# A graph network's edge stage, worked on 256 edges a step instead of 128

## The reference

```python
h  = relu(layernorm(x))
xn = layernorm(h) * ln_g + ln_b                     # 50000 x 256
q, k, v = xn @ Wq.T + bq, xn @ Wk.T + bk, xn @ Wv.T + bv
dk, dv  = silu(edge_attr @ Wdk.T + bdk), silu(edge_attr @ Wdv.T + bdv)
attn = silu(sum(q[dst] * k[src] * dk, axis=1)) * cosine_cutoff(edge_weight)
agg  = segment_sum(v[src] * dv * attn[:, None], dst)
x1   = x + h + agg @ Wo.T + bo
h1   = relu(layernorm(x1))
# graph convolution over the reversed edges with self-loops and degree norm, then a two-layer head
h7   = segment_sum((h1 @ W)[col] * norm, row) + b
out  = x1 + relu(h7 @ W1 + b1) @ W2 + b2
```

## Time and profile before

| what | value |
|---|---|
| three runs, median (lowest to highest) | 2039.34 us (2038.46 to 2040.52) |
| the profiled execution, own time | 2035.36 us |
| its span, first to last instruction | 2033.7 us |
| preparation, until the edge stage has the degree table | 0 to 118 us |
| edge stage, until its last scatter has landed | 118 to 848 us |
| second stage, until its last scatter | 848 to about 1235 us |
| node stage, overlapping it by a few steps | to 2034 us |
| busy: PE, DVE, ACT, POOL | 82%, 69%, 59%, 68% of the span |

### The profile page before, as it was taken

The page is one execution under the profiler, slowest core; times in us unless marked ns, Lnnn a source line. Parts: engine busy times, 40 slices in busy tenths (PEclk is TensorE's granted clock), DMA queues, the critical chain, the costliest instruction groups (busy, mean ns, idle before and its releaser), DMA issues.

```text
span 2033.7 us, 32020 instructions
## 1 busy us (share of the span) xinstructions
PE 1667.5 (82%) x6331; PEld 1026.7 (50%) x6331; DVE 1406.6 (69%) x5976; ACT 1193.9 (59%) x2320; POOL 1389.7 (68%) x1047
## 2 busy tenths in 40 slices
PE   4939999999999999344444541999999999999999
PEld 2315454445544545233333331676767666666666
DVE  7956666666666666355545547888888888888883
ACT  5925555554555454122222124998898989898884
POOL 2047888888888885488888877666666666666660
PEclk9959999999999999666656655999999999999999
DMA  7996555555555556244445458899999999999991
GB/s 247 418 363 204 142 146 150 140 143 143 154 140 142 145 144 203 47 87 89 89 89 90 87 102 206 234 272 273 263 272 269 269 270 268 272 269 267 266 256 72
DMA packets 170410, 391.76 MB, mean 193 GB/s; under 512 B 38847, under 2 KB 85872, under 8 KB 170368
## 3 DMA queue, kind: packets, MB, share of 16 engines
q1 hardware_dynamic: 105920, 257.96, 37.6%
q0 software_dynamic: 59552, 115.52, 31.0%
q10 hardware_dynamic: 4896, 17.83, 2.2%
HBM read 211.37 MB, written 179.85 MB: 192 GB/s over the span
## 4 chain that ended last, share of the span: by engine, by line
POOL 31%; DMA 22%; PE 18%; issue 16%; DVE 9%; SPq 2%; ACT 1%; POOLq 1%; DVEq 0%; ACTq 0%
POOL sums_dram L480 8%; DMA sums_dram<-ub,sidx 8%; POOL cg L484 7%; DMA out_dram<-cg 6%; POOL kept L567 6%; PE bank L1312 6%; PE bank L1301 6%; POOL b_rs L476 4%; DMA cg<-in_x_dram,ib 4%; PE bank L1169 3%; DVE cg L929 3%; POOL tab_d L484 3%; DMA cg<-sums_dram,ic 3%; POOL rs L476 2%; PE bank L1291 1%
## 5 line engine op out<-in xcount | busy, mean ns | idle before, releaser
L480 POOL DMA_INDIRECT sums_dram<-ub,sidx x196 | 318.9, 1627 | 96.8 <-issue 42.7
L1301 PE MATMUL bank<-kept,w 128*128 128x512 f32 x784 | 354.6, 595 | 0.0
L1312 PE MATMUL bank<-w_sb,kept 128*128 128x256 f32 x1568 | 354.3, 379 | 0.0
L567 POOL TENSOR_TENSOR kept<-kept 128x1024 f32<-128x1024 f32 x98 | 233.4, 2382 | 176.4 <-DVE cg L929 176.4
L1267 PE MATMUL bank<-cg,en 128*128 128x256 f32 x392 | 178.3, 634 | 204.4 <-ACT cg L1074 197.6
L1312 PEld LDWEIGHTS bank<-w_sb,kept 128*128 128x128 f32 x1568 | 297.9, 190 | 81.9 <-issue 46.4
L484 POOL DMA_INDIRECT cg<-in_x_dram,ib x196 | 206.3, 1052 | 78.9 <-issue 58.4
L1267 PEld LDWEIGHTS bank<-cg,en 128*128 128x128 f32 x392 | 120.5, 322 | 262.1 <-issue 236.4
L476 POOL TENSOR_TENSOR b_rs<-b_ve,minus_half 128x8 f32<-128x8 f32 x102 | 209.8, 2057 | 23.7 <-DVE b_ve L946 23.7
L476 POOL TENSOR_TENSOR rs<-ve,minus_half 128x4 f32<-128x4 f32 (+1 forms) x149 | 145.2, 974 | 101.4 <-DVE ve L781 91.6
L1301 PEld LDWEIGHTS bank<-kept,w 128*128 128x128 f32 x784 | 142.2, 191 | 141.9 <-issue 141.8
(11 more groups left out here) (183 smaller groups left out, 3227.7 us busy)
## 6 DMA issues: line engine op xcount, KB each, us to landing
sums_dram<-cg SPq DMA_DIRECT2D x162, 512.0 KB
kept<-in_x_dram SPq DMA_DIRECT2D x97, 512.0 KB, 5.8
kept<-sums_dram POOLq DMA_DIRECT2D x97, 512.0 KB, 9.9
cg<-sums_dram SPq DMA_DIRECT2D x97, 512.0 KB, 8.8
out_dram<-cg SPq DMA_DIRECT2D x97, 512.0 KB, 9.7
sums_dram<-cg ACTq DMA_DIRECT2D x34, 512.0 KB
row_d<-in_dst_dram SPq DMA_DIRECT2D x97, 64.0 KB
...
```

The source lines that it names most:

```text
L480: pool.indirect_dma_start(sums, bass.IndirectOffsetOnAxis(idx, 0), rows, None, bounds_check=last_row, compute_op=ALU.add).then_inc(done, 16)
L567: pool.tensor_tensor(X1[k.slot(8)], X[k.slot(4)], H[k.slot(2)], ALU.add).then_inc(g_xh, 1)
L1301: ins = pe.matmul(bank[:, 2 + m, :], w01[:, c, m * P:(m + 1) * P], hT[k.slot(2)][:, c * GN:(c + 1) * GN], start=(c == 0), stop=(c == KC - 1))
L1312: ins = pe.matmul(to, rT[k.slot(2)][:, c * GN + j * P:c * GN + (j + 1) * P], w2_sb[:, c, :], start=False, stop=(c == KC - 1), skip_group_c ...
```

## The change

The edge stage goes over 49 pairs (EP) of chunks instead of 98 chunks, in 49 + 7 steps instead of 98 + 11.

- POOL's program is written straight out for all 56 steps, with constant wait values. A step gathers four times 128 rows (the destination rows straight into `kept`, where they stay), raises one tile of six variances a partition to the power -0.5 (pair p-2), gathers two table entries (p-1) and issues two scatters (p-7) back to back, after both scatters of the pair before have landed. The index tile `ib` and the copies to it are gone.
- The first normalization is no longer scaled: ACT rectifies x minus its mean, the second layer norm takes that up through its variance, and x + h is formed by one instruction from the rectified rows, their scale and the rows in `kept`. So a pair has one power, after both statistics, instead of two.
- EQ of the second chunk is 256 wide: sums of the first chunk's edges take in the second chunk's messages too, and "first edge" is tested over the pair. Spare rows are two sets of 128.
- The biases sit in row 0 of the q, k, v weights: feature 0 of every normalized row is set to 1 and the row of feature 0 is subtracted from the weights of all features (a layer norm's features sum to zero). The short bias products go. The weights are changed once, in DVE's step 2.
- The edge attributes come turned from the host's array, 64 partitions of 256 edges; the turn on PE and the copy on DVE go. SP loads attributes and destination numbers once a pair, and fills `sums1` twice a pair.
- The copy of the sums out of PSUM moves from DVE to ACT, one for the pair (512 wide), and so does the copy to UB. The product with the table is formed once, behind the stage.
- ACT issues its fills eight a step instead of four. Temporary tiles of the preparation lie at the end of the room of `kept` instead of at its start.

The diff, cut to the loops (the indentation is cut too):

```diff
 assert ROWS - N >= P
-MESSAGE_STEPS = 11
...
-FILLS_STEP = 4
+FILLS_STEP = 8
...
-at0 = taken[0]
+at0 = EC * D - taken[0] - words if taken is early else taken[0]
...
-X2 = [CG[1][:, i, :].rearrange("p (a d) -> p a d", a=2) for i in range(4)]
-H2 = [CG[2][:, i, :].rearrange("p (a d) -> p a d", a=2) for i in range(4)]
+XS = [CG[1][:, i // 2, i % 2 * D:(i % 2 + 1) * D] for i in range(4)]
+G2 = [CG[2][:, i, :].rearrange("p (a d) -> p a d", a=2) for i in range(4)]
...
+    q = k.slot(2)
+    if k.within(EP):
+        wide = E - (EP - 1) * 2 * P if k.reg is None and k.off == EP - 1 else 2 * P
+        if k.past(2):
+            pass_on(sp, (m_D, k.value(-1, 2)))
+        sp.dma_start(aT[q][0:R, 0:wide], edge_attr[:, bass.ds(k.value(0, 2 * P), wide)]
+                     ).then_inc(m_attr[q], 16)
+        if k.past(2):
+            pass_on(sp, (m_eq, k.value(-1)))
+        sp.dma_start(row_d[q][:, 0:wide],
+                     dst[bass.ds(k.value(0, 2 * P), wide)].rearrange("(a e) -> a e", a=1)
+                     .broadcast_to([P, wide])).then_inc(m_row[q], 16)
...
+        for i in range(2):
+            sp.dma_start(sums1[bass.ds(k.value(0, 2 * GN) + i * GN, GN), :]
+                         .rearrange("(p j) d -> p (j d)", j=G), rows_0).then_inc(s_fill1, 16)
...
+def gather_x(p):
+    if p >= 2:
+        pool.wait_ge(m_h, p - 1)
+    for k in (2 * p, 2 * p + 1):
+        gather(XS[k % 4], x, look[:, k, 1:2], last_node, m_x[p % 2])
+        gather(kept[:, k, :], x, look[:, k, 0:1], last_node, m_x[p % 2])
+def messages(p):
+    if p < EP:
+        gather_x(p)
+    k = p - 2
+    if 0 <= k < EP:
+        if k >= 2:
+            pool.wait_ge(m_keep, k - 1)
+            pool.wait_ge(m_z, 2 * k - 2)
+        pool.wait_ge(m_ve, k + 1)
+        pool.tensor_tensor(RS[k % 2][:, :, :, :].rearrange("p a b c -> p (a b) c"),
+                           VE[k % 2][:, 1:4, :, :].rearrange("p a b c -> p (a b) c"),
+                           minus_half[:, 0:6].rearrange("p (a b) -> p a b", b=1), ALU.pow).then_inc(m_rs, 1)
+    k = p - 1
+    if 0 <= k < EP:
+        if k == 0:
             pool.wait_ge(s_table, 16)
...
+        for i in (2 * k, 2 * k + 1):
+            gather(tab_d[:, i, :], table, look[:, i, 2:3], last_entry, m_tab)
+    k = p - 7
+    if 0 <= k < EP:
+        pool.wait_ge(m_UB, k + 1)
+        pool.wait_ge(m_idx, k + 1)
+        if k >= 1:
+            pool.wait_ge(m_sc, 32 * k)
         else:
...
+            pool.wait_ge(s_fill, 16 * (NG + 1))
+        for i in range(2):
+            scatter_add(sums0, sidx[:, 2 * k + i:2 * k + i + 1], UB[2 * (k % 2) + i], m_sc)
+pool.wait_ge(m_ib, 1)
+for p in range(EP + MESSAGE_STEPS):
+    messages(p)
...
+    for i, w in enumerate((0, 512)):
+        wide = min(512, 3 * D - w)
+        for c in range(KC):
+            link(dve.tensor_tensor(qkv_w[:, c, w:w + wide], qkv_w[:, c, w:w + wide], bank[:, i, 0:wide],
+                                   ALU.subtract))
+    link(dve.tensor_tensor(qkv_w[0:1, 0, 0:2 * D], rows[:, 0:2 * D], bank[0:1, 4, :], ALU.add))
+    dve.tensor_tensor(qkv_w[0:1, 0, 2 * D:3 * D], rows[:, 2 * D:3 * D], bank[0:1, 5, 0:D],
+                      ALU.add).then_inc(s_ready, 1)
...
+    a, g, z, m = s.back(1), s.back(2), s.back(3), s.back(4)
+    if a.within(EP):
+        q = a.slot(2)
+        dve.wait_ge(m_x[q], a.turns(2, 64))
+        for i in range(2):
+            dve.bn_stats(st1[q][:, 0, i, :], XS[2 * q + i])
+        for i in range(2):
+            ins = dve.bn_stats(st1[q][:, 1, i, :], kept[:, bass.ds(a.value(0, 2) + i, 1), :]
+                               .rearrange("p a d -> p (a d)"))
+        ins.then_inc(m_st1, 1)
...
+    def key(i):
+        q = m.slot(2)
+        dve.wait_ge(m_kv, m.value(0, 2) + i + 1)
+        dve.wait_ge(m_ds, m.value(0, 2) + i + 1)
+        dve.tensor_tensor(KD[i][:, :], bank[:, 2 + i, 0:D], DS[i][:, 0:D], ALU.mult).then_inc(m_kd, 1)
...
+    def attend(i):
+        dve.wait_ge(m_q, m.value(0, 2) + i + 1)
+        dve.wait_ge(m_kd, m.value(0, 2) + i + 1)
+        dve.tensor_tensor_reduce(junk[i][:, :], bank[:, 4 + 3 * i, 0:D], KD[i][:, :], 1.0, 0.0,
+                                 ALU.mult, ALU.add, at[m.slot(2)][:, i:i + 1]).then_inc(m_at, 1)
...
+    if m.within(EP):
+        key(0)
...
+        q = z.slot(2)
+        dve.wait_ge(m_rs, z.value(1))
...
+        dve.scalar_tensor_tensor(nbz[q][:, :, :], mv2[q][:, :, :, 0], -1.0, RS[q][:, 1:3, :, 0],
+                                 ALU.mult, ALU.mult).then_inc(m_nb, 1)
...
+        pass_on(dve, (m_st1, a.value(1)))
+        for e in range(2):
+            for i in range(2):
+                ins = dve.bn_aggr(mv1[q][:, e, i, :], st1[q][:, e, i, :])
...
+    if m.within(EP):
+        attend(0)
...
+        dve.wait_ge(m_mv1, a.value(1))
...
+        dve.tensor_scalar(nm1[q][:, :, :], mv1[q][:, :, :, 0], -1.0, None, ALU.mult).then_inc(m_nm1, 1)
...
+        dve.tensor_scalar(VE[q][:, 0:2, :, 0], mv1[q][:, :, :, 1], EPS, None, ALU.add).then_inc(m_ve1, 1)
...
+        for i in range(2):
+            row = kept[:, bass.ds(z.value(0, 2) + i, 1), :].rearrange("p a d -> p (a d)")
+            ins = dve.scalar_tensor_tensor(row, G2[2 * z.slot(2) + i][:, 1, :],
+                                           RS[z.slot(2)][:, 0, i, :], row, ALU.mult, ALU.add)
+        ins.then_inc(m_keep, 1)
...
+        for i in range(2):
+            ins = dve.tensor_scalar(EQ[i][q][:, :], row_d[q][:, 0:(i + 1) * P],
+                                    dst_f[:, bass.ds(m.value(0, 2) + i, 1)], None, ALU.is_equal)
+        ins.then_inc(m_eq, 1)
...
+        dve.wait_ge(m_h, g.value(1))
+        for e in range(2):
+            for i in range(2):
+                ins = dve.bn_stats(st2[q][:, e, i, :], G2[2 * q + i][:, e, :])
...
+        dve.tensor_tensor_reduce(junk_e[0][:, 0:P], EQ[0][q][:, :], lower, 1.0, 0.0, ALU.mult, ALU.add,
+                                 cnt[q][:, 0:1])
+        dve.tensor_tensor_reduce(junk_e[1][:, :], EQ[1][q][:, :], before[:, :], 1.0, 0.0, ALU.mult, ALU.add,
+                                 cnt[q][:, 1:2]).then_inc(m_cnt, 1)
+        key(1)
...
+        pass_on(dve, (m_st2, g.value(1)))
+        for e in range(2):
+            for i in range(2):
+                ins = dve.bn_aggr(mv2[q][:, e, i, :], st2[q][:, e, i, :])
+        ins.then_inc(m_mv2, 1)
...
+        attend(1)
...
+        dve.scalar_tensor_tensor(fst[q][:, :], cnt[q][:, :], 0.5, pair_of(off_d, m), ALU.is_lt,
+                                 ALU.mult).then_inc(m_fst, 1)
...
+        dve.scalar_tensor_tensor(VE[q][:, 2:4, :, 0], VE[q][:, 0:2, :, 0], EPS, mv2[q][:, :, :, 1],
+                                 ALU.mult, ALU.add).then_inc(m_ve, 1)
...
+        dve.tensor_tensor(pair_of(sidx, m), fst[q][:, :], dump_f[:, :], ALU.add).then_inc(m_idx, 1)
...
         dve.wait_ge(m_sa, m.value(1))
...
+        dve.tensor_tensor(aa[q][:, :], sa[q][:, :], pair_of(cut, m), ALU.mult).then_inc(m_aa, 1)
         dve.wait_ge(m_aa, m.value(1))
...
+        if m.past(1):
+            dve.wait_ge(m_S, m.value(0))
+        for i in range(2):
+            dve.scalar_tensor_tensor(MSG[i][:, :], bank[:, 2 + i, D:2 * D], aa[q][:, i:i + 1],
+                                     DS[i][:, D:2 * D], ALU.mult, ALU.mult).then_inc(m_msg, 1)
...
+    if s.back(4).within(EP):
+        turned(0)
...
+    if k.within(EP):
         act.wait_ge(m_U, k.value(1))
...
+        act.activation(UB4[:, 2 * k.slot(2):2 * k.slot(2) + 2, :].rearrange("p a d -> p (a d)"),
+                       bank[:, 6, :], ACT.Copy).then_inc(m_UB, 1)
...
+    if s.back(4).within(EP):
+        silu_d(0)
...
+        act.wait_ge(m_nb, k.value(1))
...
+        for e in range(2):
+            ins = act.activation(Z2[i][:, e, 1:D], G2[2 * q + i][:, e, 1:D], ACT.Identity,
+                                 bias=nbz[q][:, e, i:i + 1], scale=RS[q][:, 1 + e, i, :])
...
+    if s.back(3).within(EP):
+        scaled(0)
+    if s.back(4).within(EP):
+        turned(1)
+    if s.back(3).within(EP):
+        scaled(1)
...
+        act.wait_ge(m_nm1, k.value(1))
...
+        for i in range(2):
+            act.activation(G2[2 * q + i][:, 0, :], XS[2 * q + i], ACT.Relu, bias=nm1[q][:, 0, i:i + 1])
+            ins = act.activation(G2[2 * q + i][:, 1, :], kept[:, bass.ds(k.value(0, 2) + i, 1), :]
+                                 .rearrange("p a d -> p (a d)"), ACT.Relu, bias=nm1[q][:, 1, i:i + 1])
+        ins.then_inc(m_h, 1)
+    if s.back(4).within(EP):
+        silu_d(1)
...
+    if k.within(EP):
+        act.wait_ge(m_S, k.value(1))
...
+        act.activation(ST[k.slot(2)][:, :, :, :].rearrange("p a k e -> p (a k e)"), bank[:, 5, :],
+                       ACT.Copy).then_inc(m_ST, 1)
...
+    if k.within(EP):
+        act.wait_ge(m_at, k.value(1, 2))
         if k.past(2):
             act.wait_ge(m_aa, k.value(-1))
         act.activation(sa[k.slot(2)][:, :], at[k.slot(2)][:, :], ACT.Silu).then_inc(m_sa, 1)
...
+    m = s.back(4)
+    f = s.back(5)
+    u = s.back(6)
```

(33 more changed lines are left out.)

447 lines of the change are left out of this document (165 added, 282 removed).

## The result

The changed kernel takes 2007.76 us (median of four runs, 2005.75 to 2008.78) against 2038.9 us: ratio 0.9845, 95% interval 0.9828 to 0.9862, 31 us less. The forecast was 57 us less, a median of 1982. The profiled execution took 2008.08 us (span 2006.4) where the sum said 1978.6, so 29.5 us are to be found.

What follows compares the result with a forecast made beforehand. POOL's queue was taken as the bound: 13.2 us a pair over 40 steady steps (528 us), plus ramp and tail, gave 56.8 us less, 1978.6, and 4.0 for the median: 1982 us. Own range 1964 to 2000; stated range 1962 to 2027.

Steps and rivals of the forecast that it cites:

- rival A: Edge stage: POOL's power waits for variances in the two-step loop; 13.9 us a step, about 2011 us; chance 0.19.
- POOL's queue as the bound: Edge stage: POOL's instructions and the idle time ahead of them set the step, 13.2 us a pair (12.8 to 13.9).
- The others keep up: Edge stage: PE needs 11.6 us a pair, ACT about 8.5, the two-step loop 12.6 a step, all under 13.2.
- The loop over two steps: Edge stage: gathers, landing, DVE's variances, POOL's power, tables, scatters, next gathers; 25.1 us for two steps, 12.6 a step.
- The 0.30 us ahead of an indirect DMA: POOL's edge stage: this idle time stays when the program is written straight out; unrolling is worth nothing.
- Rival C: Edge stage: POOL's idle 0.30 us shrinks to 0.05, PE becomes the bound at 11.6 us, about 1916 us; chance 0.06.
- Rival B: Edge stage: PE's standstills lower its granted clock; at 0.77 the step is 15.0 us, about 2056 us, slower; chance 0.12.
- The ramp term: Start of the edge stage, up to the first pair's scatters, out at 200: costs 13 us (bounds 0 and 25).
- The degree table is there at 117.8: Start of the edge stage: time the table is available, read from the profile before; POOL's step 2 starts at about 120.5.
- The tail term: End of the edge stage: from POOL's last gathers at 728.6 to the second stage's first gather at 791.4, 62.8 us.
- two scatters and their landing: End of the edge stage, behind the last message and its sums: scatters 3.8 us, landing 3.0 us.
- Second and node stage keep their time: Stages behind the edge stage: lengths unchanged, 367.9 and 757.5 us; a change over 5 us makes the forecast wrong.

Runs made afterwards that it cites:

- Experiment 6: The changed kernel with its power of six numbers a pair issued as two, of four and of two numbers: 2017.74 us, ratio 0.9913 to the kernel before.
- the small product of experiment 7: The changed kernel with one extra, overwritten PE product of 256 columns ahead of every chunk's query product: 2005.69 us, ratio 0.9846 to the kernel before.
- experiment 9: The kernel before the change with POOL's edge stage written out, 109 steps, in place of a loop: 2036.92 us, ratio 1.0003.
- Experiment 1: The changed kernel with the last 34 fills of `sums0` issued by SP instead of ACT: 1997.07 us, ratio 0.9783 to the kernel before.
- experiment 2: The changed kernel with SP's last four pairs of `sums1` fills spread out, one pair a step: 2008.58 us, ratio 0.9842 to the kernel before.
- experiment 3: The changed kernel with the copy and scatter of the sums one step earlier: 1995.92 us, ratio 0.9795 to the kernel before.
- experiments 3 to 5: Besides experiment 3, the changed kernel with DVE's node loop not set to a 256-slot block (2002.99 us), or with 209 semaphore increments at DVE's start (2006.01 us).

## Why the prediction was right, and where it was not

**POOL's queue as the bound: right, and the size too.** 13.2 us forecast, 13.2 measured. Counted as in the forecast, with the idle time ahead, the gathers took 5.4 (forecast 5.3), the power 1.4 (1.5, chosen between two sizes), the tables 2.6 (2.6), the scatters 3.9 (3.8): the sum is right to a tenth because the small errors cancel. Experiment 6 lengthens POOL's pair and the steps follow; the small product of experiment 7 lengthens PE's and they don't. That the time lies in the stated range owes something to luck, though: it is outside the forecast's own 1964 to 2000 and 3 us from the 2011 of rival A, whose mechanism the rows do not show. The room kept for A's slower steps took in errors at the ends that no rival named.

**The others keep up: right, by more than forecast for PE.** PE needs 10.9 a pair where I had 11.6. Which of PE's terms was too large, no run separates. The loop over two steps was not the pace in the steady part; without the table gathers the rows point to it, at 22.5 us, where my 25.1 less the tables' 2.6 makes 22.5 as well.

**The 0.30 us ahead of an indirect DMA: right.** It stands in the written-out program as it did in the loop, and experiment 9 puts a zero behind the written-out form. By the rule of the Trainium skill cited there the step would have been shorter; here it was not. Rival C falls.

**Rival A falls:** POOL's power waited 0.7 us in 400. **Rival B falls as to time:** PE's granted clock did dip to 0.95 to 0.98 in the stretches of 300 to 700 us, and in the small product's run, with PE busier, it was 1.00 in the same stretches at the same step. The dip cost nothing here. PE did wait for ACT's turned rows in each step, up to 2.9 us; the waits that the section of the Trainium skill cited for B tells of are longer, so it did not speak for B.

**The ramp term was too small: 26 us, not 13.** "ACT, which issues eight fills ahead of its other work in that step" took one such step; there were two, each of 7 to 8 us, and both stood between PE and its turned rows. And the start of the whole stage, "The degree table is there at 117.8", was taken over from before, though eight fills a step now stood right behind its write on the queues. 6.6 of the 13.2 us come from there. Experiment 1 gives 13.5 us back in sum: 5.9 of the table, 5.4 of the first long wait and 3.6 of a later one, less 1.4 in small pieces; the second long wait stays, now for another reason.

**The tail term was too small by 7.3 us.** PE was faster than forecast there, the last message came 48.4 us behind the last gathers and not 53.1. But "two scatters and their landing" behind it was one pair; three pairs were still to be scattered, 6.4 us each with the landing of the one before, so 21.7 us in place of 9.7. This is read from the rows. The burst of fills looked like the culprit, and spreading it gave nothing (experiment 2); scattering one step earlier gave 2.6 us and left three pairs in a row (experiment 3).

**"Second and node stage keep their time" failed.** They lost 8.9 us together, over the 5 us that I had named as the mark of a wrong forecast. 5.9 of it is one stall of DVE that comes and goes with the place of its code (experiments 3 to 5). The 2.9 us of the second stage are not explained; its length was 366.4 to 375.3 us in kernels that do not differ there, so I would not read a cause into them.

## What to carry to other kernels

Where one queue was the pace, its instructions and the idle time ahead of them, added up, gave the steady step here to a tenth of a microsecond; what went wrong were the ends. Count there, step by step, every instruction that stands ahead of the first results (DMA issues on a compute engine above all), what else is on the DMA engines when the first input is written, and how many serialized transfers are left after the last result. A change to one stage also moves the code of later ones, so compare the untouched stages too.
